# Gated graph stage: the gate by ScalarE's sigmoid, and abs, exp and log for the other half alone

## The reference, cut to what matters

```
N, E, D = 3125, 50000, 128           # nodes, edges (sorted by dst), features
z    = concat(x[dst], x[src], edge_attr)          # E x 384
gate = sigmoid(z @ W_f + b_f)                     # E x 128
core = softplus(z @ W_s + b_s)                    # E x 128
agg  = segment_sum(gate * core, dst)              # N x 128
x    = layernorm(x + (x + agg))
```

## Time and profile before

| | us |
|---|---|
| median of 3 runs | 3386.99 (3385.04 to 3388.22) |
| the profiled execution, whole | 3393.63 |
| its span (first to last instruction) | 3391.9 |
| gated stage: from the third block's `core` to the last block's | 1391.12 to 1902.37 |
| busy over the span: PE, DVE, ACT, POOL | 3124.6, 1349.3, 1381.1, 866.8 |
| mean granted clock of PE | 0.937 |

### The profile page before, as it was taken

How to read it: one execution, slowest core, us unless ns; L and a number is a source line. 1 busy time by engine, 2 the same in 40 slices (tenths; PEclk the granted TensorE clock), 3 DMA queues, 4 the chain that set the end, 5 groups by cost and what they waited for, 6 DMA issues and landing times. The chain is left out here.

```text
span 3391.9 us, 43780 instructions
## 1 busy us (share of the span) xinstructions
PE 3124.6 (92%) x13945; PEld 2044.2 (60%) x13945; DVE 1349.3 (40%) x3224; ACT 1381.1 (41%) x2450; POOL 866.8 (26%) x935
## 2 busy tenths in 40 slices
PE   5888999968988897799999799999999999999998
PEld 4775555547877886577777555555555555555554
DVE  6991110125666667799999711101110000000012
ACT  4870000224555555788888522222222222222233
POOL 2000000027777770677777200000000000000000
PEclk8998999977787777899999899999999999999999
DMA  2556677623333330676666557666666767667674
GB/s 65 207 207 247 273 288 304 260 76 78 83 84 81 79 72 26 175 192 183 183 181 183 184 240 296 272 284 279 272 272 279 289 283 297 281 272 286 284 297 172
DMA packets 163325, 709.38 MB, mean 209 GB/s; under 512 B 36427, under 2 KB 129482, under 8 KB 150055
## 3 DMA queue, kind: packets, MB, share of 16 engines
q1 hardware_dynamic: 125964, 619.72, 46.6%
q0 software_dynamic: 33920, 84.12, 10.4%
q10 hardware_dynamic: 3224, 2.75, 0.3%
HBM read 658.10 MB, written 48.07 MB: 208 GB/s over the span
## 5 line engine op out<-in xcount | busy, mean ns | idle before, releaser
L1363 PE MATMUL deep_out_psum<-deep_adjacency,deep_scaled_nodes_odd 125*128 125x450 f32 (+1 forms) x1750 | 669.7, 537 | 0.0
L1363 PE MATMUL deep_out_psum<-deep_adjacency,deep_scaled_nodes 125*128 125x450 f32 (+1 forms) x1750 | 669.7, 537 | 0.0
L1603 POOL DMA_INDIRECT source_rows<-gat_source_rows,pair_src x416 | 415.4, 999 | 578.7 <-POOLq L62 452.2
L1363 PEld LDWEIGHTS deep_out_psum<-deep_adjacency,deep_scaled_nodes_odd 125*128 125x128 f32 x1750 | 328.4, 189 | 312.0 <-issue 312.0
L1363 PEld LDWEIGHTS deep_out_psum<-deep_adjacency,deep_scaled_nodes 125*128 125x128 f32 x1750 | 328.1, 189 | 310.7 <-issue 310.7
L2171 POOL DMA_INDIRECT near_room<-gate_source_rows,pair_src x416 | 398.6, 958 | 224.4 <-issue 126.2
L1421 ACT ACTIVATE deep_squares<-deep_aggregate,deep_vectors 128x450 f32<-128x450 f32 (+1 forms) x70 | 46.8, 668 | 618.0 <-DVE deep_aggregate L1488 618.0
L2216 PE MATMUL gate_core_psum<-edge_weights,edge_features_t 128*128 128x256 f32 x832 | 259.7, 393 | 39.5 <-ACT edge_features_t L2250 39.5
L1363 PE MATMUL gcn_out_psum<-adjacency_columns,gcn_scaled_nodes 125*128 125x450 f32 (+1 forms) x700 | 268.2, 537 | 0.0
L1499 DVE SCALAR_TENSOR_TENSOR deep_normed<-deep_aggregate,deep_vectors,deep_squares 128x450 f32<-128x450 f32 (+1 forms) x70 | 47.9, 684 | 531.8 <-ACT deep_squares L1429 531.8
L1641 PE MATMUL score_terms_psum<-ident,source_rows 128*128 128x128 f32 x416 | 144.8, 348 | 70.6 <-issue 54.1
(11 more groups left out here) (404 smaller groups left out, 4552.9 us busy)
## 6 DMA issues: line engine op xcount, KB each, us to landing
deep_adjacency<-adjacency SPq DMA_DIRECT2D x69, 5625.0 KB, 16.2
adjacency_columns<-adjacency SPq DMA_DIRECT2D x19, 5625.0 KB, 16.1
adjacency<-adjacency_columns SPq DMA_DIRECT2D x7, 5625.0 KB, 17.6
edge_features<-in_edge_attr_dram SPq DMA_DIRECT2D x416, 64.0 KB
att_node_rows<-pair_dst_rows SPq DMA_DIRECT2D x104, 125.0 KB
gate_node_rows<-pair_dst_rows SPq DMA_DIRECT2D x104, 125.0 KB
source_rows<-gat_source_rows,pair_src POOLq DMA_INDIRECT x416
near_room<-gate_source_rows,pair_src POOLq DMA_INDIRECT x416
```

Source lines behind the costliest of these rows:

```text
L1363: m = nc.tensor.matmul(op[:, n % 2, 0:cols], h[l % 2][:, s, :], ring[0:T, n % 2, s, 0:cols], start=s == 0, stop=s == NS - 1)
L1603: pool.indirect_dma_start(xj[:, b % HOLD, q, :], None, d["h_r"], bass.IndirectOffsetOnAxis(ap=c["pair_src"][:, b * PQ + q:b * PQ + q + 1], ...
```

## The change

The gate comes from ACT's sigmoid, in place, in one pass over the gate half of z (128 x 512, scale -1 since that half is negated). Abs, exp and log run over the core half alone (128 x 512) into a tile of its own in SBUF with two buffers, and `softplus` is done on that half alone and in place. Sigmoid is in another of ACT's function tables than exp and log, so ACT's program has table loads: an even block loads sigmoid's, runs `gate`, loads log's, and runs abs, exp and log; an odd block runs these three first, then loads sigmoid's and runs `gate`.

z moves to a tile of its own with three buffers. Since log and gate no longer write to PSUM, `core(b)` waits for `add(b-2)` and no longer for `message(b-3)`, with two PSUM buffers in place of three; the freed PSUM gives two buffers to the transposed edges and two to the pair sums. `add(b)` now waits for `message(b-3)`. DVE's order becomes `add(b+1)`, `onehots(b+2)`, `softplus(b-1)`, `message(b-1)`, `merge(b-1)`. PE's order of steps isn't changed.

```diff
-        z = wide[:, N:N + 2 * PQ * W].rearrange("p (k q f) -> p k q f", k=2, q=PQ)
-        ab = sb("gate_core_abs", [128, PQ, W])
-        sp_ = sb("gate_core_softplus", [128, PQ, W])
+        CORES, ZS = 2, 3
+        z = sb("gate_core", [128, ZS, PQ, W])
+        ab = sb("gate_core_abs", [128, 2, PQ, D])
...
             def core(b):
...
                 if b >= CORES:
-                    pe.wait_ge(s_msg, b - CORES + 1)
+                    pe.wait_ge(s_zr, b - CORES + 1)
...
             def gate(b):
-                act.wait_ge(s_sp, b + 1)
-                nc.scalar.activation(gate_of(b), sp_[:, :, 0:D], ACT.Exp, scale=-1.0).then_inc(s_gt, 1)
+                nc.scalar.activation(z[:, b % ZS, :, 0:D], z[:, b % ZS, :, 0:D], ACT.Sigmoid, scale=-1.0).then_inc(s_gt, 1)
+
+            def log(b):
+                a = ab[:, b % 2, :, :]
+                if b >= 2:
+                    act.wait_ge(s_sp, b - 1)
+                nc.scalar.activation(a, z[:, b % ZS, :, D:W], ACT.Abs).then_inc(s_ab, 1)
+                act.wait_ge(s_ab, b + 1)
+                nc.scalar.activation(a, a, ACT.Exp, scale=-1.0).then_inc(s_ex, 1)
+                act.wait_ge(s_ex, b + 1)
+                nc.scalar.activation(a, a, ACT.Ln, bias=1.0).then_inc(s_ln, 1)
...
             for b in range(NPB):
                 act.wait_ge(s_zr, b + 1)
...
+                if b % 2 == 0:
+                    nc.scalar.preload_act_table_set("sigmoid_and_friends")
+                    gate(b)
+                    nc.scalar.preload_act_table_set(LOG_EXP)
+                    log(b)
+                else:
+                    log(b)
+                    nc.scalar.preload_act_table_set("sigmoid_and_friends")
+                    gate(b)
                 if b + 2 < NPB:
                     copy_edges(b + 2)
-            gate(NPB - 1)
...
             for b in range(NPB):
-                if b >= 1:
-                    softplus(b - 1)
+                if b + 1 < NPB:
+                    add(b + 1)
                 if b + 2 < NPB:
                     onehots(b + 2)
                 if b >= 1:
+                    softplus(b - 1)
                     message(b - 1)
-                if b + 1 < NPB:
-                    add(b + 1)
-                if b >= 1:
                     merge(b - 1)
```

More of the change, by code:

```diff
@@ L2201, in transposes @@
                 pe.wait_ge(s_e[b % 4], 16 * PQ * (b // 4 + 1))
-                if b >= 1:
-                    pe.wait_ge(s_et, b)
+                if b >= 2:
+                    pe.wait_ge(s_et, b - 1)
                 for q in range(PQ):
-                    m = nc.tensor.transpose(p_e[:, q * 128:(q + 1) * 128], e_n[:, b % 4, q, :], c["ident"][:, :])
+                    m = nc.tensor.transpose(p_e[:, b % 2, q * 128:(q + 1) * 128], e_n[:, b % 4, q, :], c["ident"][:, :])
                 m.then_inc(s_eT, 1)
@@ L2223, in scatter @@
                 pe.wait_ge(s_msg, b + 1)
-                if b >= 1:
-                    pe.wait_ge(s_O, PQ * b)
+                if b >= 2:
+                    pe.wait_ge(s_O, PQ * (b - 1))
                 for q in range(PQ):
-                    m = nc.tensor.matmul(p_a[:, q * T:(q + 1) * T], msg[:, b % 2, q, :], oh[:, b % 4, q, :], start=True, stop=True)
+                    m = nc.tensor.matmul(p_a[:, b % 2, q * T:(q + 1) * T], msg[:, b % 2, q, :], oh[:, b % 4, q, :], start=True, stop=True)
                 m.then_inc(s_A, 1)
@@ L2243, in _ @@
         def _(act):
-            nc.scalar.preload_act_table_set(LOG_EXP)
+            nc.scalar.preload_act_table_set("sigmoid_and_friends")
             def copy_edges(b):
@@ L2249, in copy_edges @@
                     act.wait_ge(s_z, b - 1)
-                nc.scalar.copy(e_t[:, b % 2, :], p_e[:, :]).then_inc(s_et, 1)
+                nc.scalar.copy(e_t[:, b % 2, :], p_e[:, b % 2, :]).then_inc(s_et, 1)
             def gate(b):
-                act.wait_ge(s_sp, b + 1)
-                nc.scalar.activation(gate_of(b), sp_[:, :, 0:D], ACT.Exp, scale=-1.0).then_inc(s_gt, 1)
+                nc.scalar.activation(z[:, b % ZS, :, 0:D], z[:, b % ZS, :, 0:D], ACT.Sigmoid, scale=-1.0).then_inc(s_gt, 1)
+            def log(b):
+                a = ab[:, b % 2, :, :]
+                if b >= 2:
+                    act.wait_ge(s_sp, b - 1)
[4 more added lines that the diff above has]
+                nc.scalar.activation(a, a, ACT.Ln, bias=1.0).then_inc(s_ln, 1)
             copy_edges(0)
@@ L2292, in add @@
                 dve.wait_ge(s_g[b % 4], 16 * PQ * (b // 4 + 1))
-                if b >= 2:
-                    dve.wait_ge(s_sp, b - 1)
-                vec.tensor_tensor(z[:, b % 2, :, :], core_of(b), xj[:, b % 4, :, :], ALU.add).then_inc(s_zr, 1)
+                if b >= ZS:
+                    dve.wait_ge(s_msg, b - ZS + 1)
+                vec.tensor_tensor(z[:, b % ZS, :, :], core_of(b), xj[:, b % 4, :, :], ALU.add).then_inc(s_zr, 1)
             def softplus(b):
                 dve.wait_ge(s_ln, b + 1)
-                if b >= 1:
-                    dve.wait_ge(s_msg, b)
-                vec.scalar_tensor_tensor(sp_[:, :, :], z[:, b % 2, :, :], 0.0, core_of(b), ALU.max, ALU.add).then_inc(s_sp, 1)
+                vec.scalar_tensor_tensor(z[:, b % ZS, :, D:W], z[:, b % ZS, :, D:W], 0.0, ab[:, b % 2, :, :], ALU.max, ALU.add).then_inc(s_sp, 1)
             def message(b):
                 dve.wait_ge(s_gt, b + 1)
+                dve.wait_ge(s_sp, b + 1)
                 dve.wait_ge(s_oh, b + 1)
@@ L2307, in message @@
                     dve.wait_ge(s_A, b - 1)
-                vec.tensor_tensor(msg[:, b % 2, :, :], gate_of(b), sp_[:, :, D:W], ALU.mult).then_inc(s_msg, 1)
+                vec.tensor_tensor(msg[:, b % 2, :, :], z[:, b % ZS, :, 0:D], z[:, b % ZS, :, D:W], ALU.mult).then_inc(s_msg, 1)
             def merge(b):
@@ L2316, in merge @@
                     o = (odd if q % 2 else c["h_t"])[:, bass.ds(node[q], T)]
-                    vec.tensor_tensor(o, o, p_a[:, q * T:(q + 1) * T], ALU.add).then_inc(s_O, 1)
+                    vec.tensor_tensor(o, o, p_a[:, b % 2, q * T:(q + 1) * T], ALU.add).then_inc(s_O, 1)
                 for j, (c0, n) in enumerate(SPANS):
```

9 lines of the change are left out of this document (2 added, 7 removed).

## The result

| | before | changed |
|---|---|---|
| median of 4 runs, us | 3386.01 | 3758.69 (3757.34 to 3763.09) |
| ratio to before, 95% interval | | 1.1102 (1.1087 to 1.1118) |
| span of the profiled execution, us | 3391.9 | 3761.0 |
| one block of the stage, `add` to `add`, mean, us | 5.06 | 8.74 |
| mean granted clock of PE | 0.937 | 0.916 |

The kernel became 11% slower. All of it lies in the gated stage: `add` of block 2 starts at 1395.67 and that of block 103 at 2277.97, which is 101 blocks of 8.74 us. 101 x (8.74 - 5.06) = 372 us, against 369 us between the two spans.

A forecast was written before the change was run, and what follows sets the result against it. PE, DVE and POOL were taken to run side by side near a 5.06 us period. A serial cycle of 7.81 us, with clock falls 9.1, over 101 blocks plus 2 us at the start gave 3797 us, range 3655 to 3880.

The forecast's parts named there:

- The large term: Gated stage: DVE's new order makes a serial cycle with PE, 7.81 us a block against 5.06, adding 278 us.
- The width of `softplus`: DVE's half-wide softplus takes 0.68 us in place of 1.21, bounds 0.60 and 1.21.
- The table loads: ACT: three loads to two blocks at 1283 ns, 1.92 us a block, hidden under the longer period.
- rival 4: Gated stage not slower, POOL's gathers bound it at 5.0 us a block: 3382 or 3377 us; chance 0.06.
- The clock: PE's 3.1 us gap makes its clock fall repeatedly, 1.7 us a fall, taking the period from 7.81 to 9.1 us.
- Rival 1: Gated stage: same serial cycle but PE's clock holds at 2.4 GHz, 3667 us; chance 0.14.
- POOL's 5.0 us: Gated stage: four gathers of 0.95 + 0.30 us a block, the bound if the change isn't slower.
- start and tail: Start of the gated stage adds 2 us through block 0's longer ACT round; the 16.5 us tail stays.

The follow-up runs named there:

- e1: Changed kernel with DVE's old order put back (softplus, onehots, message, add, merge), all else kept: 3397.15 us, ratio 1.0036 to the kernel before.
- e2: Changed kernel with DVE's new order kept, PE's scatter and DVE's merge moved one round later: 3415.89 us, ratio 1.0086 to the kernel before.
- e9: Changed kernel with DVE's onehots moved behind message, run on a slower chip: 3853.37 us, ratio 1.0011 to the kernel before there.
- e4: Changed kernel without its 156 table loads, gate an exp of the same size (values not the reference's): 3754.37 us, ratio 1.1092 to the kernel before.
- e3: Changed kernel with eight filler matmuls on PE ahead of each block's transposes: 3665.23 us, ratio 1.0822 to the kernel before.
- e7: Changed kernel with DVE's onehots moved behind message, run on a slower chip: 3848.68 us, ratio 1.0010 to the kernel before there.
- e12: Changed kernel with DVE's old order and no load at the head of even blocks: 3404.69 us, ratio 1.0052 to the kernel before.
- e10: Kernel before with only DVE's order changed, message behind add and onehots, on a slower chip: 3891.71 us, ratio 1.0133 to the kernel before there.
- e5: Changed kernel with DVE's old order, no table loads, exp as gate, on a slower chip: 3818.82 us, ratio 0.9948 to the kernel before there.
- e11: Changed kernel with DVE's old order, no load at the head of even blocks, slower chip: 3830.34 us, ratio 0.9980 to the kernel before there.
- e6: Changed kernel with DVE's old order, no load at the head of even blocks, slower chip: 3831.64 us, ratio 0.9971 to the kernel before there.

## Why the prediction was right

**The large term.** The prediction set the cycle at 7.81 us at 2.4 GHz; it is 7.76. Its steps one by one: `add` to the one-hots 1.14, the two one-hots 0.26 and 0.59, `softplus` 0.69 with 0.08 behind it, `message` 0.69, the semaphore to PE 0.06, the scatter 0.99 to the next matmul, and `core` 3.26 to the next `add`. The largest miss is `core`, with 0.09 less than the 3.32 and 0.03 of the prediction. The width of `softplus`, for which bounds of 0.60 and 1.21 stood, is 0.69. e1, e2 and the timeline of e9 show that it is this cycle and that its steps add.

**What it costed at nothing.** The table loads (3 to two blocks, 1283 ns each, the one for the table already in place included) were to be hidden. e4 shows it. The 7.0 us of ACT's time that the prediction worked out for rival 4 from the Trainium skill's figure counts three switches to two blocks, where only two of the three loads change the table; and the trace has no idle time behind a load (one starts at 1802.92 and takes 1.28, the next pass starts at 1804.21).

**The clock.** That it would fall again and again in gaps of 3.1 us was right, as was the cost of one fall, 1.67 us measured for 1.7. Its frequency was the term that was mis-sized: the middle between one fall a block and one in two gave 0.75 a block and 1.29 us; it is 57 in 101, and 0.98 us. The 0.31 us over 101 blocks are 31 us, and with the 5 us of the cycle they are nearly all of the distance from 3797 to 3759. The middle between two guesses had no row behind it, so that it came this close is in part luck. Rival 1, the clock that holds, is e3: 3665 us measured for 3667. The Trainium skill ("TensorE: Matmul & The Clock Gate", on why this matters for your kernels) asks for no gaps above about 3 us; here the same gap of 3.11 us came with a fall in 57 rounds and with none in 44, a gap of 2.26 us with one in 14 of 101 rounds in e7 and in 47 of 101 in e9, the same kernel, and one of 1.3 us in e3 with none. So the length of the gap alone doesn't tell how often the clock falls; what does stays open.

**What was off.** The prediction named POOL's 5.0 us as a fixed floor for rival 4. It isn't fixed: e1, e2 and e12 have gathers of 998, 1034 and 1045 ns where the kernel before had 956. And its start and tail were put at +2 us together; the span's difference of 369 is 3 us under the rounds' 372, within what these reads can tell.

## What to carry to other kernels

Where two in-order engines hand work back and forth in software pipelining, write down for each step on one engine which step of the other must be over first, and look for an instruction that waits for the newest block standing ahead of one that serves an older block which the other engine needs before it can go on. Here a shorter softplus and looser buffers gained nothing, since DVE's wait for the newest `core` had come to stand ahead of the message that PE's next `core` needed, and that is worth the sum of all steps between. A gap made in this way on TensorE is paid twice, as its work behind the gap may run at half the clock.

## What the runs showed of the hardware

**POOL's gathers get longer beside DVE instructions whose two operands are both in SBUF.** The groups of the gather's line, 1450 to 1850 us, of the kernel before, e1, e2 and e12, in this order (count, busy us, mean ns, idle):

```profile
L2171 POOL DMA_INDIRECT near_room<-gate_source_rows,pair_src x318 | 304.2, 956 | 97.0 <-issue 97.0
```

```profile
L2167 POOL DMA_INDIRECT near_room<-gate_source_rows,pair_src x308 | 307.4, 998 | 93.8 <-issue 93.8
```

```profile
L2167 POOL DMA_INDIRECT near_room<-gate_source_rows,pair_src x300 | 310.1, 1034 | 91.4 <-issue 91.4
```

```profile
L2167 POOL DMA_INDIRECT near_room<-gate_source_rows,pair_src x297 | 310.4, 1045 | 90.6 <-issue 90.0 <-DVE gate_core L2298 0.6
```

A gather alone takes 0.95. In the changed kernel's round above, the first gather runs beside the one-hot and `softplus`, the second beside `message`, the third beside nothing on DVE until 1804.53:

```profile
1801.22 1.40 POOL L2167 DMA_INDIRECT near_room<-gate_source_rows,pair_src  x1 [4.14 <-DVE gate_core L2299]
...
1802.93 1.07 POOL L2167 DMA_INDIRECT near_room<-gate_source_rows,pair_src  x1 [0.31 <-issue]
...
1804.31 0.94 POOL L2167 DMA_INDIRECT near_room<-gate_source_rows,pair_src  x1 [0.30 <-issue]
```

In the kernel before, `softplus` and `message` read one operand from PSUM, and the 132 gathers of that stretch beside one of them alone took 0.94 to 0.96; the change moved both operands to SBUF. The one-hot comparison has both there in either kernel. In e10, where `softplus` and `message` still read from PSUM, 98 of 398 gathers take 1.39 to 1.41, and they are just those that start beside it:

```profile
2103.79 0.67 DVE L2287 TENSOR_TENSOR gate_node_onehot<-ramp,pair_dst_local 128x500 f32<-128x500 f32 x1
2103.89 1.40 POOL L2171 DMA_INDIRECT near_room<-gate_source_rows,pair_src  x1 [2.27 <-DVE wide_room L2295]
```

The gather ends 0.83 us after the comparison does. So it is with the two longer ones above: 0.82 us after the one-hot (1801.80) and after `message` (1803.18). It holds for all 194 gathers over 1.0 us in the changed kernel's stage, all 98 of e10 and all 12 of 317 in the kernel before, for 107 of 111 in e12 and 52 of 62 in e1. An instruction that starts only after the gather mostly leaves it at 0.95, as `softplus` does in e1. So both the operands and the order of the steps decide which gathers are held up. The Trainium skill ("GPSIMD Engine Reference", specifications) says that GpSimd shares its SBUF interfaces with VectorE and contends with instructions of two SBUF inputs, which fits these rows. All of this is read from traces; no run changed the place of an operand alone. At 4 x (1.045 + 0.304) = 5.4 us a block it is what e12 ran into. It isn't what e2 lost against e1: there the gathers end 14 us ahead of their `add`.

**Chips differ.** On the two chips of e5 to e11 the attention stage moves about 60 GB/s where it moves about 80 on the others, and the gated stage begins 220 us later. In e5, e6 and e11 the gated stage also stands still, for 2 to 7.5 us in about every third block. In e5, from 1700 to 2100 us:

```profile
DVE h_t L2317 <- remote: 100.0, 19, 7.5
```

DVE waits there ahead of the first merge of a block, for nothing that the profile can name, and the other engines wait for DVE. In e7 to e10, on the same chips, no round is longer than 8.9 us. From the last `add` on, the program takes the same time as elsewhere. What it is stays open. Late gathered rows, which the expectations of e9 name, are not it: in e5, e6, e7, e9 and e11 the last gather of a block ends at least 14 us ahead of its `add`. A comparison of kernels with this stage is only of use beside the kernel before on the same chip, and even then such a chip can hide a loss: e7's cycle is 6.91 us a block where the kernel before has 5.06 on the first kind, and its ratio there is 1.001. The changed kernel itself wasn't run on one.
